# The end of an attention step moved into the next step, and the odd query stacks copied on ScalarE

## The chip, the cores and the metric

The kernel runs on one core of a Trainium2 chip. Its time is the time on the device in microseconds (us). TensorE is called PE here, as in the profile, VectorE DVE, ScalarE ACT, GpSimd POOL and SyncE SP. Each takes its own instructions in their order and waits on semaphores for the others. All DMAs of this kernel are issued by SP.

## The reference

Eight batches of 256 tokens with 128 features go through an adaptive layer norm, an attention block in overlapping windows with a small MLP, a second adaptive layer norm and a soft mixture of eight experts. Cut to what matters here, the attention of one batch is:

```python
x = layernorm(hidden_states, ln1_g, ln1_b)
q, k, v = heads(x @ wq + bq), heads(x @ wk + bk), heads(x @ wv + bv)   # 16 heads of 8
for i in range(0, S, 32):                                              # 8 windows
    start, end = max(0, i - 16), min(S, i + 48)
    attn = softmax(q[:, start:end] * 8 ** -0.5 @ k[:, start:end].T)
    wo = attn @ v[:, start:end]
    out[:, start:end] = blend(out, wo)                                 # linear ramps where windows overlap
out = merge_heads(out) @ wproj + bproj + residual
```

## The kernel before

**Stages.** After a start (modulation of the norm, loads), a loop `step(b)` over the eight batches computes attention on all engines at once; every engine has its own `step(b)`, written by hand as a list of calls. Then come the MLP of all tokens and the experts, which the change leaves alone (from about 216 us on in the profile).

**Scores.** A window has up to 64 tokens. The 16 heads are split in two row groups of the PE array (`par`), the windows in even and odd ones (`eo`), the tokens in two halves (`sel`): eight groups g of 16 small matmuls. q and k are cut into three bf16 parts and stacked as 48 rows, six products of parts at once. The stacks `qst[b % 3][eo]` and `kst[b % 3]` are made by a way through DRAM: ACT copies q and k out of PSUM (`copy_qk`, lines 716 to 722), DVE cuts them into `parts` (`cut_qk`, lines 1063 to 1068), SP writes the parts to `stack_scratch` (`write_parts`, line 266) and reads them back as stacks (`read_stacks`, line 277): two DMAs each for even queries, keys and odd queries. The even and the odd query stack hold the same numbers; they are two because the rows with the maxima differ.

**Two passes.** `scores_a(b, g)` (line 392) computes scores from which DVE takes the negative maxima (`maxima`, line 1073). `cut_m` on POOL cuts these into two bf16 parts, `transpose_m` on PE (line 415) turns them, `copy_mt` on DVE (line 1079) takes them out of PSUM, and `write_mrow` on SP (line 285) writes them with four DMAs as two further rows of the query stack. `scores_b(b, g)` (line 407) computes the transposed scores with the maxima already off; ACT takes `exp` (line 740), `probs_v` (line 430) multiplies with V, `copy_pv` (line 746), `turn_sums` (line 440) and `normalise` on DVE (lines 1087 to 1095) divide by the sums, `gather_context` (line 450) puts the windows together, ACT copies the context (line 803), `project_out` (line 457) projects it and `attention_out` (line 1102) adds the residual. In PE's step b the calls `a(g)` are `scores_a(b + 1, g)`.

**What is ahead of what.** In step b PE turns and projects batch b + 3 (`transpose_x`, `project_qk`, w0b and w1b), and V of batch b + 2 (`project_v`, line 371). The scores of pass a use the banks psa[0] and psa[1] in turn; psa[0] also takes `transpose_m(b, 1)`, so that `scores_a(b + 1, 0)` waits for `mt_ready`. w1b is shared by `project_qk`, `transpose_m(b, 0)`, the gather and the projection. `keep_busy` issues filler matmuls on constants. The end of PE's step before is:

```python
turn_sums(b, 1)
keep_busy(5)
gather_context(b)
scores_b(b + 1, 1)
project_out(b)
```

## Time and profile before

| | us |
|---|---|
| median of 3 runs | 343.5 |
| the runs | 335.82, 343.5, 345.52 |
| the profiled execution | 340.69 |
| its span | 338.9 |
| PE busy in it | 284.3 (84%) |
| DVE, ACT, POOL busy | 224.2, 141.1, 75.3 |

The span runs from the first to the last instruction; the profiled execution's own time is 1.8 us more. Rows of the profile name a line of the kernel, an engine, what it writes and reads, and how often. A busy PE is not PE at its peak; PEclk is the clock it was granted, as a share of 2.4 GHz. Of a row of matmuls that follow each other the start of the next one tells the time it took, since their ends overlap.

### The profile page before, as it was taken

How to read it: one execution, taken by the hardware profiler on the slowest of the kernel's cores; microseconds unless marked ns; L12 is line 12 of the kernel's file. 1: busy time of each engine (PE TensorE's matmuls, PEld its weight loads, DVE VectorE, ACT ScalarE, POOL GpSimd, SP SyncE). 2: the span in 40 equal slices, each digit the busy share in tenths (PEclk: the TensorE clock that was granted, in tenths of full speed). 3: DMA queues.
4: the chain of work that ended last, by engine and by line, in shares of the span. 5: the costliest groups of instructions: out<-in, count | busy, mean ns of one | idle time of the engine just before them, and what ended most of it. 6: DMA issues, size and time to landing. Idle time of an engine off the chain costs nothing.

```text
span 338.9 us, 10357 instructions
## 1 busy us (share of the span) xinstructions
PE 284.3 (84%) x4168; PEld 223.3 (66%) x4168; DVE 224.2 (66%) x634; ACT 141.1 (42%) x282; POOL 75.3 (22%) x116
## 2 busy tenths in 40 slices
PE   4865479599897988969998899887899989999992
PEld 2323356387775766747876787565697779778992
DVE  7554764466758376452645626498857898798986
ACT  1343136328354462734226235654536216624220
POOL 5453240311403141000101010215540024003020
PEclk9775558859789796995558557999989999999999
DMA  6107752377617365271710340000000000101011
GB/s 183 43 0 202 167 120 47 106 164 174 172 35 177 92 122 150 52 186 35 142 22 6 120 143 3 0 2 0 0 2 1 0 2 0 32 2 31 2 32 32
DMA packets 21902, 23.71 MB, mean 70 GB/s; under 512 B 3296, under 2 KB 18528, under 8 KB 21856
## 3 DMA queue, kind: packets, MB, share of 16 engines
q1 hardware_dynamic: 21856, 23.06, 27.2%
q8 instruction: 33, 0.54, 0.7%
q14 instruction: 13, 0.11, 0.1%
HBM read 14.67 MB, written 8.13 MB: 67 GB/s over the span
## 4 chain that ended last, share of the span: by engine, by line
PE 47%; DVE 17%; issue 9%; SPq 8%; DMA 8%; ACT 7%; POOL 2%; ACTq 0%; DVEq 0%; POOLq 0%
PE bank L655 6%; SPq L285 5%; PE bank L407 5%; PE bank L450 4%; DMA qst<-mt 4%; PE bank L371 4%; PE bank L430 3%; PE bank L392 3%; DVE xh L1032 3%; PE bank L440 3%; PE bank L637 3%; PE bank L639 3%; PE bank L638 3%; DVE acc L1371 2%; DMA vmsk<-in_vmask 2%
## 5 line engine op out<-in xcount | busy, mean ns | idle before, releaser
L1073 DVE TENSOR_REDUCE nm<-bank 128x8 f32<-128x512 f32 x64 | 43.6, 688 | 28.3 <-PE bank L392 28.2
L878 POOL TENSOR_TENSOR rs<-ve,mhalf 128x2 f32<-128x2 f32 (+1 forms) x24 | 19.4, 810 | 137.4 <-DVE ve L1029 130.6
L740 ACT ACTIVATE prob<-bank 128x512 f32<-128x512 f32 x64 | 36.6, 600 | 29.1 <-PE bank L407 28.6
L392 PE MATMUL bank<-kst,qst 48*64 48x64 bf16 x1024 | 32.5, 213 | 6.4 <-issue 4.3
L830 ACT ACTIVATE sg<-bank 128x512 f32<-128x512 f32 x32 | 18.9, 601 | 43.5 <-PE bank L639 42.0
L655 PEld LDWEIGHTS bank<-wds,hh 128*128 128x128 f32 x256 | 32.3, 191 | 7.0 <-issue 5.4
L655 PE MATMUL bank<-wds,hh 128*128 128x128 f32 x256 | 33.7, 277 | 2.8 <-DVE acc L1371 2.3
L392 PEld LDWEIGHTS bank<-kst,qst 48*64 48x64 bf16 x1024 | 25.4, 125 | 16.0 <-issue 13.3
L407 PE MATMUL bank<-qst,kst 50*64 50x64 bf16 x1024 | 31.0, 213 | 3.9 <-DMA qst<-mt 3.5
L430 PE MATMUL bank<-prob,vb 128*32 128x64 f32 x1024 | 27.8, 258 | 7.6 <-issue 4.7
L1371 DVE SCALAR_TENSOR_TENSOR acc<-bank,rt,acc 128x128 f32<-128x128 f32 x112 | 32.6, 341 | 1.2
L407 PEld LDWEIGHTS bank<-qst,kst 50*64 50x64 bf16 x1024 | 24.7, 125 | 10.4 <-DMA qst<-mt 4.8
L637 PE MATMUL bank<-h3rest,wpart 128*128 128x512 f32 x64 | 27.5, 430 | 0.8 <-ACT sg L830 0.8
L430 PEld LDWEIGHTS bank<-prob,vb 128*32 128x32 f32 x1024 | 21.3, 130 | 10.4 <-issue 5.7
L1273 DVE TENSOR_TENSOR hh<-sg,bank 128x512 f32<-128x512 f32 x32 | 21.8, 682 | 6.6 <-ACT sg L830 5.8
L639 PE MATMUL bank<-h3part,wpart 128*128 128x512 f32 x64 | 25.1, 393 | 0.0
L638 PE MATMUL bank<-h3part,wrest 128*128 128x512 f32 x64 | 25.1, 392 | 0.0
L347 PE MATMUL bank<-ones 128*128 128x256 bf16 x100 | 22.7, 371 | 2.6 <-issue 2.6
L614 PEld LDWEIGHTS bank<-w2s,gt 128*128 128x128 f32 x128 | 17.9, 209 | 7.1 <-issue 5.0
L1032 DVE TENSOR_SCALAR xh<-xs,mv,rs 128x128 f32<-128x128 f32 x32 | 15.7, 535 | 6.6 <-POOL rs L878 6.6
L614 PE MATMUL bank<-w2s,gt 128*128 128x128 f32 x128 | 18.4, 295 | 1.0 <-DVE comb L1242 1.0
L1102 DVE TENSOR_TENSOR res<-bank,res 128x256 f32<-128x256 f32 x8 | 3.4, 425 | 23.7 <-PE bank L457 23.7
(140 smaller groups left out, 498.8 us busy)
## 6 DMA issues: line engine op xcount, KB each, us to landing
qst<-stack_scratch SPq DMA_DIRECT2D x32, 216.0 KB, 4.8
stack_scratch<-parts SPq DMA_DIRECT2D x16, 216.0 KB, 2.5
kst<-stack_scratch SPq DMA_DIRECT2D x16, 216.0 KB, 5.0
stack_scratch<-parts SPq DMA_DIRECT2D x16, 144.0 KB, 2.4
stack_scratch<-parts SPq DMA_DIRECT2D x16, 72.0 KB, 2.1
qst<-mt SPq DMA_DIRECT2D x64, 4.0 KB
out_x<-fin SPq DMA_DIRECT2D x4, 256.0 KB, 2.3
xs<-in_x SPq DMA_DIRECT2D x1, 896.0 KB, 7.2
```

Of the source, the lines that this page charges most:

```text
L392: m = pe.matmul(psa[g % 2][WIN * half:WIN * half + WIN, WIN * h2:WIN * h2 + WIN], qst[n][eo][rows_, h2, at:at + WIN], kst[n][rows_, h2, at ...
L407: m = pe.matmul(bank[WIN * half:WIN * half + WIN, WIN * h2:WIN * h2 + WIN], kst[n][rows_, h2, at:at + WIN], qst[n][eo][rows_, h2, at:at + ...
L430: m = pe.matmul(psv[32 * ct:32 * ct + 32, at:at + WIN], vb[n][:, eo, H2 * par + h2, sel, :, :], prob[par][:, h2, sel, :], start=True, stop ...
L614: m = pe.matmul(bk[6][:, k * P:(k + 1) * P], gt[:, c, k * P:(k + 1) * P], w2s[:, c, :], start=(c == 0 and k == 0), stop=(c == FF - 1), ski ...
L637: pe.matmul(bank[:], wpart[:, w, e, :], tokens_rest, start=True, stop=False)
L638: pe.matmul(bank[:], wrest[:, w, e, :], tokens, start=False, stop=False)
L639: return pe.matmul(bank[:], wpart[:, w, e, :], tokens, start=False, stop=True)
L655: m = pe.matmul(bk[4 + e % 2][:, k * P:(k + 1) * P], hh[e][:, k * P:(k + 1) * P], wds[:, e, :], start=True, stop=True)
L740: act.activation(prob[g // 2 % 2][:, :, g % 2, :], psb[g % 2][:].rearrange("p (h q) -> p h q", h=H2), ACT.Exp).then_inc(exp_done, 1)
L1032: return dve.tensor_scalar(dst, src, mean, r, ALU.subtract, ALU.mult)
L1073: dve.tensor_reduce(nm[:, g, :], psa[g % 2][:].rearrange("p (h k) -> p h k", h=H2), AX_X, ALU.max, negate=True).then_inc(max_done, 1)
L1371: dve.scalar_tensor_tensor(out=acc[:, k, :], in0=src, scalar=w, in1=acc[:, k, :], op0=ALU.mult, op1=ALU.add).then_inc(acc_step, 1)
```

## The change

It moves `gather_context(b)`, the copy of the context, `project_out(b)` and `attention_out(b)` from the end of step b into step b + 1 (and behind the loop for the last batch). `project_v` is done one batch ahead instead of two, in the middle of the step, `transpose_x(b + 3)` and `project_qk(b + 3)` come later, `copy_qk(b + 3)` becomes ACT's last call of the step and `cut_qk(b + 3)` DVE's last. SP writes the parts one step later, and sends the second half's maxima rows ahead of the stack reads. The odd query stack is not read from the scratch: ACT copies it from the even one in two pieces (`copy_odd`), for which DVE fills 32 rows of each even stack with zeros at the start, three fills more. Some waits of PE that were repeated in each group are made once. Fillers go from 9 to 6 in a step.

The diff, without the declaration of the semaphore:

```diff
@@ -269,8 +270,7 @@
                 n = b % DEEP
                 if b >= DEEP:
                     sp.wait_ge(b_done, after(b_done, 8 * (b - DEEP + 1)))
-                for k, stack, written in ((0, qst[n][0], q_written), (1, kst[n], k_written),
-                                          (0, qst[n][1], q_written)):
+                for k, stack, written in ((0, qst[n][0], q_written), (1, kst[n], k_written)):
                     sp.wait_ge(written, after(written, 48 * (b + 1)))
                     rows_of = scr[b, k].rearrange("t (d h) n -> (t d) h n", h=NH)
                     for r in range(2):
@@ -298,7 +298,7 @@
                 sp.dma_start(dst[:], src).then_inc(small_loaded, 16)
 
             write_parts(0)
-            sp.wait_ge(ones_ready, after(ones_ready, 2 * DEEP))
+            sp.wait_ge(ones_ready, after(ones_ready, 3 * DEEP))
             read_stacks(0)
             write_parts(1)
             write_mrow(0, 0)
@@ -315,16 +315,12 @@
 
             def step(b):
                 write_mrow(b, 1)
-                if b == 0:
-                    write_parts(2)
-                elif b + 2 < B:
-                    read_stacks(b + 2)
+                if b + 2 < B:
+                    write_parts(b + 2)
                 if b + 1 < B:
                     write_mrow(b + 1, 0)
-                if b == 0:
-                    read_stacks(2)
-                if b + 3 < B:
-                    write_parts(b + 3)
+                if b + 2 < B:
+                    read_stacks(b + 2)
                 if b == B - 2:
                     load_late()
 
@@ -379,11 +375,13 @@
 
             def scores_a(b, g):
 
-                pe.wait_ge(stack_ready, after(stack_ready, 96 * (b + 1)))
                 if g == 0:
+                    pe.wait_ge(stack_ready, after(stack_ready, 64 * (b + 1)))
                     pe.wait_ge(mt_ready, after(mt_ready, 2 * b))
                 else:
                     pe.wait_ge(max_done, after(max_done, 8 * b + g - 1))
+                if g == 4:
+                    pe.wait_ge(odd_ready, after(odd_ready, 2 * (b + 1)))
                 par, halves = spans(g)
                 eo, n = g // 4, b % DEEP
                 rows_ = slice(64 * par, 64 * par + ROWS)
@@ -396,7 +394,8 @@
 
             def scores_b(b, g):
 
-                pe.wait_ge(mrow_ready, after(mrow_ready, 128 * b + 64 * (g // 4 + 1)))
+                if g % 4 == 0:
+                    pe.wait_ge(mrow_ready, after(mrow_ready, 128 * b + 64 * (g // 4 + 1)))
                 if g:
                     pe.wait_ge(exp_done, after(exp_done, 8 * b + g - 1))
                 par, halves = spans(g)
@@ -419,7 +418,8 @@
             def probs_v(b, gp):
                 n = b % 2
                 pe.wait_ge(exp_done, after(exp_done, 8 * b + 2 * gp + 2))
-                pe.wait_ge(v_ready, after(v_ready, 4 * (b + 1)))
+                if gp == 0:
+                    pe.wait_ge(v_ready, after(v_ready, 4 * (b + 1)))
                 eo, par = gp // 2, gp % 2
                 if par == 0:
                     pe.wait_ge(pvs_ready, after(pvs_ready, 2 * b + eo))
@@ -521,17 +521,14 @@
             transpose_x(2)
             for g in range(5, 8):
                 scores_a(0, g)
+            keep_busy(6)
+            scores_b(0, 0)
+            scores_b(0, 1)
             pe.wait_ge(mt_ready, after(mt_ready, 1))
             project_qk(2)
-            pe.wait_ge(qk_ready, after(qk_ready, 12))
-            project_v(1, 0)
-            project_v(1, 1)
-            keep_busy(10)
-            scores_b(0, 0)
-            scores_b(0, 1)
 
             def step(b):
-                ahead, prep, values = b + 1 < B, b + 3 < B, b + 2 < B
+                ahead, prep = b + 1 < B, b + 3 < B
 
                 def a(g):
                     if ahead:
@@ -543,41 +540,42 @@
                 probs_v(b, 0)
                 scores_b(b, 3)
                 a(0)
-                keep_busy(2)
+                if b + 2 < B:
+                    pe.wait_ge(qk_ready, after(qk_ready, 4 * (b + 3)))
+                if b:
+                    gather_context(b - 1)
+                if ahead:
+                    project_v(b + 1, 0)
+                    project_v(b + 1, 1)
+                else:
+                    turn_tokens(0)
                 a(1)
+                probs_v(b, 1)
+                if b:
+                    project_out(b - 1)
+                scores_b(b, 4)
+                a(2)
+                scores_b(b, 5)
+                a(3)
+                turn_sums(b, 0)
+                if ahead:
+                    keep_busy(3)
                 if prep:
                     pe.wait_ge(v_ready, after(v_ready, 4 * (b + 2)))
                     transpose_x(b + 3)
-                a(2)
-                if not ahead:
-                    turn_tokens(0)
-                probs_v(b, 1)
-                if prep:
-                    pe.wait_ge(att_ready, after(att_ready, b))
-                    project_qk(b + 3)
-                a(3)
-                scores_b(b, 4)
-                scores_b(b, 5)
-                turn_sums(b, 0)
-                keep_busy(2)
                 a(4)
+                pe.wait_ge(att_ready, after(att_ready, b))
                 if ahead:
-                    if prep:
-                        pe.wait_ge(qk_ready, after(qk_ready, 4 * (b + 4)))
-                    else:
-                        pe.wait_ge(att_ready, after(att_ready, b))
                     transpose_m(b + 1, 0, w1b)
                 else:
                     turn_tokens(1)
                 probs_v(b, 2)
                 scores_b(b, 6)
-                if values:
-                    pe.wait_ge(v_ready, after(v_ready, 4 * (b + 2)))
-                    project_v(b + 2, 0)
                 a(5)
+                if prep:
+                    pe.wait_ge(mt_ready, after(mt_ready, 2 * b + 3))
+                    project_qk(b + 3)
                 scores_b(b, 7)
-                if values:
-                    project_v(b + 2, 1)
                 a(6)
                 if not ahead:
                     turn_tokens(2)
@@ -587,23 +585,19 @@
                 else:
                     pe.wait_ge(late_loaded, after(late_loaded, 128))
                     first(0, 0)
+                a(7)
+                turn_sums(b, 1)
                 if ahead:
-                    pe.wait_ge(mt_ready, after(mt_ready, 2 * b + 3))
+                    keep_busy(3)
+                    scores_b(b + 1, 1)
                 else:
                     first(0, 1)
-                    pe.wait_ge(att_ready, after(att_ready, b))
-                a(7)
-                turn_sums(b, 1)
-                keep_busy(5)
-                gather_context(b)
-                if ahead:
-                    scores_b(b + 1, 1)
-                else:
-                    first(0, 2)
-                project_out(b)
 
             for b in range(B):
                 step(b)
+            gather_context(B - 1)
+            first(0, 2)
+            project_out(B - 1)
 
             def second(g, c):
 
@@ -739,6 +733,19 @@
                 act.wait_ge(pv_done, after(pv_done, 4 * b + g // 2 - 1))
                 act.activation(prob[g // 2 % 2][:, :, g % 2, :], psb[g % 2][:].rearrange("p (h q) -> p h q", h=H2),
                                ACT.Exp).then_inc(exp_done, 1)
+
+            def copy_odd(b, half):
+
+                act.wait_ge(stack_ready, after(stack_ready, 64 * (b + 1)))
+                heads = slice(H2 // 2 * half, H2 // 2 * (half + 1))
+                even, odd = [qst[b % DEEP][eo][0:64 + ROWS, heads, LINE - S:LINE] for eo in range(2)]
+                act.activation(odd, even, ACT.Copy).then_inc(odd_ready, 1)
+
+            def copy_ctxt(b):
+                act.wait_ge(ctx_done, after(ctx_done, b + 1))
+                act.wait_ge(proj_done, after(proj_done, b))
+                act.activation(ctxt[:], w1b[:, PAD:PAD + S], ACT.Identity, bias=col[:, BV:BV + 1]
+                               ).then_inc(ctxt_ready, 1)
 
             def copy_pv(b, eo):
                 act.wait_ge(pv_done, after(pv_done, 4 * b + 2 * eo + 2))
@@ -770,25 +777,31 @@
             copy_qk(1)
             copy_mod(7, bk[1])
             copy_v(0)
+            copy_odd(0, 0)
+            copy_odd(0, 1)
             copy_xt(2)
-            copy_qk(2)
-            copy_v(1)
             exp(0, 0)
             exp(0, 1)
+            copy_qk(2)
 
             def step(b):
                 ahead, prep = b + 1 < B, b + 3 < B
                 exp(b, 2)
+                if b:
+                    copy_ctxt(b - 1)
                 exp(b, 3)
-                if prep:
-                    copy_xt(b + 3)
                 if not ahead:
                     copy_h2t(0)
                 copy_pv(b, 0)
+                if ahead:
+                    copy_odd(b + 1, 0)
+                exp(b, 4)
+                if ahead:
+                    copy_v(b + 1)
+                    copy_odd(b + 1, 1)
+                exp(b, 5)
                 if prep:
-                    copy_qk(b + 3)
-                exp(b, 4)
-                exp(b, 5)
+                    copy_xt(b + 3)
                 if not ahead:
                     copy_h2t(1)
                 exp(b, 6)
@@ -796,19 +809,15 @@
                 copy_pv(b, 1)
                 if not ahead:
                     copy_h2t(2)
-                if ahead:
+                else:
                     exp(b + 1, 0)
-                act.wait_ge(ctx_done, after(ctx_done, b + 1))
-                act.wait_ge(proj_done, after(proj_done, b))
-                act.activation(ctxt[:], w1b[:, PAD:PAD + S], ACT.Identity, bias=col[:, BV:BV + 1]
-                               ).then_inc(ctxt_ready, 1)
-                if ahead:
                     exp(b + 1, 1)
-                if b + 2 < B:
-                    copy_v(b + 2)
+                if prep:
+                    copy_qk(b + 3)
 
             for b in range(B):
                 step(b)
+            copy_ctxt(B - 1)
 
             def copy_h3t(g, bank):
                 act.wait_ge(t3_done, after(t3_done, g + 1))
@@ -958,13 +967,13 @@
                     cut_m(b + 1, 0)
                 if group is not None:
                     root_tokens(group)
-                if b + 3 < B:
-                    copy_x1v(b + 3)
                 if b + 4 < B:
                     norm_x(b + 4)
                     second_root_x(b + 4)
                 if b + 1 < B:
                     cut_m(b + 1, 1)
+                if b + 3 < B:
+                    copy_x1v(b + 3)
 
             for b in range(B):
                 step(b)
@@ -1134,6 +1143,7 @@
             for n in range(DEEP):
                 for par in range(2):
                     dve.memset(kst[n][64 * par + 32:64 * par + 64].bitcast(F32), TWO_ONES).then_inc(ones_ready, 1)
+                dve.memset(qst[n][0][32:64].bitcast(F32), 0.0).then_inc(ones_ready, 1)
 
             dve.wait_ge(sc_exp, after(sc_exp, 1))
             dve.tensor_scalar(sce[:, 1, :], sce[:, 0, :], 1.0, None, ALU.add).then_inc(sc_step, 1)
@@ -1196,41 +1206,41 @@
                 copy_mt(b, 1)
                 maxima_next(0)
                 maxima_next(1)
+                if b:
+                    attention_out(b - 1)
                 if norm:
                     ln_a(b + 4)
+                if group is not None:
+                    ln2_stats(group)
                 maxima_next(2)
                 if norm:
                     ln_b(b + 4)
                 maxima_next(3)
-                if group is not None:
-                    ln2_stats(group)
                 normalise(b, 0)
                 if ahead:
                     copy_mt(b + 1, 0)
                 maxima_next(4)
-                if prep:
-                    cut_qk(b + 3, 0)
-                maxima_next(5)
-                if prep:
-                    cut_qk(b + 3, 1)
                 if group is not None:
                     normed_tokens(group)
-                maxima_next(6)
+                maxima_next(5)
                 if not ahead:
                     gate(GA)
                 if norm:
                     ln_c(b + 4)
+                maxima_next(6)
                 maxima_next(7)
                 normalise(b, 1)
                 if norm:
                     ln_d(b + 4)
-                attention_out(b)
-                if not ahead:
-                    ln2_stats(NG - 1)
+                if prep:
+                    cut_qk(b + 3, 0)
+                    cut_qk(b + 3, 1)
 
             for b in range(B):
                 step(b)
 
+            attention_out(B - 1)
+            ln2_stats(NG - 1)
             normed_tokens(NG - 1)
             gate(GB)
```

## Rows read from the trace of the kernel before

**Rows 1.** Windows by step: us; busy PE, PEld, DVE, ACT, POOL; PEclk; DMA share; GB/s

```profile
54.90:78.10 23.20, 18.47 (x442) 14.62 (x438) 12.79 (x34) 9.33 (x21) 4.79 (x10) 0.78 0.51 123
78.10:158.50 80.40, 68.52 (x1730) 53.86 (x1729) 48.92 (x123) 40.66 (x91) 16.45 (x35) 0.86 0.49 119
158.50:179.40 20.90, 20.37 (x427) 16.63 (x425) 10.43 (x30) 7.05 (x14) 1.92 (x5) 0.56 0.34 68
179.40:199.00 19.60, 17.61 (x429) 14.32 (x422) 10.76 (x31) 7.02 (x14) 1.93 (x5) 0.61 0.33 108
```

**Rows 2.** The page: granted clock in 40 equal slices of the span, in tenths

```profile
PEclk9775558859789796995558557999989999999999
```

**Rows 3.** Timeline of PE in step 2: start us, us, engine, line, tiles, [idle before it]

```profile
104.80 0.65 PE L430 MATMUL bank<-prob,vb 128*32 128x64 f32 x32 [0.58 <-ACT prob L740]
105.38 0.44 PE L407 MATMUL bank<-qst,kst 50*64 50x64 bf16 x16
105.75 0.71 PE L371 MATMUL bank<-wa,x1v 128*128 128x128 f32 x4
...
110.55 0.47 PE L430 MATMUL bank<-prob,vb 128*32 128x64 f32 x17 [2.20 <-issue]
...
113.49 2.08 PE L450 MATMUL bank<-idf,ctxn 128*128 128x128 f32 x8
...
116.13 0.71 PE L457 MATMUL bank<-wa,ctxt 128*128 128x128 f32 x4 [0.15 <-ACT ctxt L803]
```

**Rows 4.** Timeline of PE in steps 5 and 6, at the lower clock

```profile
161.97 1.08 PE L430 MATMUL bank<-prob,vb 128*32 128x64 f32 x32
...
168.09 0.63 PE L407 MATMUL bank<-qst,kst 50*64 50x64 bf16 x16
168.65 1.22 PE L371 MATMUL bank<-wa,x1v 128*128 128x128 f32 x4
```

**Rows 5.** The chain of waits in order of time: start us, us, what

```profile
4.99 6.84 DMA vmsk<-in_vmask
...
201.76 1.77 DMA qst<-mt
...
213.69 1.16 PE bank L450 x8
```

**Rows 6.** Timeline of DVE, start, batch 2's cut and step 2

```profile
9.30 0.29 DVE L1055 COPY scb<-sce 128x256 f32<-128x256 f32 x1
...
48.98 0.76 DVE L1063 TENSOR_TENSOR qkr<-qk,parts 128x576 f32<-128x576 f32 x1 [2.36 <-ACT parts L722]
...
50.27 0.76 DVE L1068 TENSOR_TENSOR parts<-qkr,parts 128x576 bf16<-128x576 f32 x1
...
97.59 0.28 DVE L1079 COPY mt<-bank 32x256 bf16<-32x256 bf16 x1 [0.16 <-PE bank L415]
```

**Rows 7.** Timeline of SP's issues in step 2

```profile
97.89 2.69 SPq L285 DMA_DIRECT2D qst<-mt  x4
...
103.10 0.88 SPq L277 DMA_DIRECT2D qst<-stack_scratch  x2
...
108.75 3.04 SPq L266 DMA_DIRECT2D stack_scratch<-parts  x6
```

**Rows 8.** Groups by line and form: count, busy us, mean ns, idle ahead of them

```profile
L734 ACT ACTIVATE vb<-bank 64x256 f32<-64x256 f32 x32 | 12.0, 376 | 4.4 <-PE bank L371 3.8
...
L746 ACT ACTIVATE pvs<-bank 128x512 f32<-128x512 f32 x16 | 9.6, 597 | 20.5 <-PE bank L430 20.5
...
L1136 DVE MEMSET kst<- 32x1152 f32 x6 | 6.1, 1018 | 2.5 <-issue 1.5 <-PEq L1475 1.0
```

**Rows 9.** Timeline of ScalarE in step 2, the copies of q and k

```profile
102.09 0.50 ACT L716 ACTIVATE qk<-bank,bqs 128x288 f32<-128x288 f32 x1 [0.89 <-PE bank L363]
...
103.26 0.51 ACT L722 ACTIVATE parts<-bank,col 128x288 bf16<-128x288 f32 x1
```

**Rows 10.** DMA issues by line: KB each, median us to landing

```profile
qst<-stack_scratch SPq DMA_DIRECT2D x32, 216.0 KB, 4.8
```

1 line of the change is left out of this document (added).

## The prediction

> **What bounds the kernel now.** I read first the busy shares by step and then the orders of the queues inside one step. The table of windows [rows 1] cuts the attention loop at the starts of `transpose_m(b,1)`: step 0 takes 23.2 us, steps 1 to 4 take 80.4, 20.1 each, step 5 takes 20.9 and step 6 takes 19.6. PE is busy 80 to 97% of these rows while no other engine reaches 65%, and its granted clock is 0.56 to 0.86 on the mean: it falls towards 1.2 GHz again and again [rows 1, 2]. So a step is PE's fixed order of work, and what lengthens it is any wait in that order and the clock that is lost after it.
>
> The rows of one step show both. Back to back at 2.4 GHz a score group starts 0.37 after the one before, `probs_v` takes 0.58, a half of `project_v` 0.64 [rows 3]; the same at 1.2 GHz take 0.56, 1.0 and 1.15 [rows 4], and the gather 1.16 against 2.08 [rows 3, 5]. In step 2 PE stands still for 2.20 before 110.55, and the gather at 113.49 runs at the lower clock [rows 3]. That tail (turn the sums, divide, gather, copy, project) is a chain through four engines with 9 filler matmuls per step beside it.
>
> Two transfers bind the order of a step. A half of the maxima goes `transpose_m`, `copy_mt` on DVE (0.28) [rows 6], four DMA issues in a row on SP (2.69) [rows 7], 1.77 to land [rows 5], then `scores_b`. From the start of `copy_mt` that is 0.28 + 2.69 + 1.77 + about 0.05 for hand-overs = 4.8 us.
>
> **The change, part by part.**
>
> *The tail.* The gather and output projection of step b-1 leave the end and stand between `a(0)` and `scores_b(b,4)`. What stood alone on PE there was gather, context copy wait and projection, 1.16 + 0.5 + 0.64 at 2.4 GHz; from 110.55 to the next step 6.6 us passed in step 2 [rows 3]. Now the tail after `scores_b(b+1,0)` is `a(7)`, sums, three fillers, `scores_b(b+1,1)`, about 1.7 us.
>
> *What comes in the way: the cut of q and k.* Before, ScalarE copied qk(b+3) in mid-step and DVE cut it between maxima. Now `copy_qk(b+3)` stands behind `exp(b+1,1)`, the last exponential of the step, and both `cut_qk` calls are DVE's last work of the step. DVE's next instruction is `copy_mt(b+1,1)`. It is queued behind the cut, and behind it wait `a(0)` of step b+1, since bank psa[0] comes free only with `mt_ready`, and on SP the maxima rows for `scores_b(b+1,4)`. The exponential takes 0.6, as the copy of the same 512 columns [rows 8]. The four copies of `copy_qk` take from 102.09 to 103.77, 1.7 [rows 9]. The cut takes from 48.98 to 51.03, 2.05 [rows 6]. With 0.1 of hand-overs, `copy_mt` starts 4.45 after the end of `scores_b(b+1,1)` and ends at 4.75. PE has `scores_b(b+1,2)`, `transpose_m`, `probs_v`, `scores_b(b+1,3)` for this time, 0.37 + 0.16 + 0.58 + 0.37 = 1.5, and stands still for about 3.1. This falls in steps 0 to 5, since batches 2 to 7 are cut so.
>
> *The new step.* Let `a(0)` start at 0, with `copy_mt` just ended.
> - PE to `scores_b(b,4)`: 0.37 + 1.16 + 1.28 + 0.37 + 0.58 + 0.64 = 4.4. The maxima rows: 2.69 + 1.77 + 0.05 = 4.5. So 4.5; the moved work is hidden exactly, at 2.4 GHz. At 1.2 GHz it is 0.56 + 2.0 + 2.3 + 0.56 + 1.0 + 1.15 = 7.6 and not hidden.
> - ScalarE then has in a row: `exp(b,4)`, `copy_v` (4 x 0.39 apart, about 1.6), `copy_odd` second half, and `a(4)` waits for this copy. The odd copy of 4 heads by 256 columns is 1,024 elements in bf16; the trace has none of that size. Copies of 256 take 376 ns and of 512 take 597 [rows 8], a slope of 0.86 ns: 1.04 us. Bounds: 0.8, if it were two copies of 512 that start as close together as those of `copy_qk`, 0.39 [rows 9]; and 1.5, four copies of 256 without overlap. I take 1.0, the line through the two sizes, since only source and destination change. `scores_b(b,4)` ends at 4.9; 4.9 (the first half ends at 5.3) + 0.5 + 1.6 + 1.0 = 8.4 for `a(4)`. PE gets there with b(4), a(2), b(5), a(3), sums, fillers and the transposes of x at about 7.3, so a second stop of 1.1.
> - `transpose_m(b+1,0)` 0.4 later, 0.25 to its result and 4.8 of copy and rows: `scores_b(b+1,0)` at 13.9. PE's own work there is 4.4 and one exponential, so a stop of about 0.7.
> - tail of 1.7 to `scores_b(b+1,1)`, its own 0.37: 16.0. Then 4.75 as above: 20.7.
>
> So even at full clock a step takes 20.7, as long as now (20.1).
>
> *The clock.* Each step now has one gap of 3.1 us and stops of 1.1 and 0.7. In the trace a gap of 2.20 was enough for the gather at 113.49 to run at 1.2 GHz [rows 3], and steps 5 and 6, with least work, stand at 0.56 and 0.61 [rows 1]; in step 2 it is back for the projection at 116.13. I take the lower clock for the stretch after the gap, up to `scores_b(b,4)`: 7.6 instead of 4.5, +3.1, of which 0.2 goes back into shorter stops. Forecast 23.6 a step. Bounds: 20.7 with the clock up throughout; all at 1.2 GHz 7.6 to `scores_b(b,4)`, 3.6 over ScalarE to `a(4)`, 7.5 of PE work to `scores_b(b+1,0)`, 3.2 to the end of `scores_b(b+1,1)` and 4.7 for copy and cut: 26.6.
> The Trainium skill, "TensorE: Matmul & The Clock Gate", section "HAM oscillation — how this bites in real kernels", tells of a kernel in which a DMA wait that recurs in every tile makes TensorE pay its warm-up again in every tile. It speaks against this change: by it each of these steps would be a 23.6 one, without it each 20.7. The trace of before agrees in that every step has a stretch at half clock.
>
> *Odd stacks not read.* Two of six stack reads per batch go, 2 x 216 KB [rows 10] and 0.9 us of SP issue [rows 7] each time. They lie beside other work, since the reads are a step ahead. At the start it counts, where the first score group waits for all six: 0.9 of issue, and about as much in the landing, as a third of what is under way goes; I book -1.8.
>
> *Order on SP.* `write_parts(b+2)` (3.04 of issue [rows 7]) stands between the two rows groups: SP is free again 6.1 after `a(0)`, the second group's maxima are there at 9.4. No cost. The stack reads follow at 12.1 to 13.9 and land 4.8 later [rows 10], 2 us ahead of the next `a(0)`; only behind step 5, where no cut delays `a(0)`, would they be 1.1 late. Dropped PE waits and the later `copy_x1v` cost nothing: what they waited for is long done in each case.
>
> *The start.* DVE gets three more fills of 32x1152. One takes 1.02, and the six of before have 2.5 of idle ahead of them [rows 8], 1.0 of it ahead of the first, so 0.3 each: 3.9 us. `spread_sc` at 9.30 [rows 6], which feeds the first modulation matmul, slips by it. Some of that was covered by a wait for a load that ended at 11.83 [rows 5]; I book +2.9. With the -1.8 above: +1.1. Bounds 0 and +3.9.
>
> **The sum.** Profiled execution: 340.7 (span 338.9 and 1.8 around it).
> - start: +1.1
> - step 0: no gather in it, 20.4 at full clock, 22.5 with part at half, against 23.2 from one `copy_mt` to the next: -0.7
> - steps 1 to 4: 4 x (23.6 - 20.1) = +14.0
> - steps 5 to 7: without the cut behind them 18.9 and 17.8 at full clock, 22.7 at half; they were mostly at half and are of equal work (one gather and one `project_v` more, 15 fillers less): +0.5
>
> 355.6. The median shown (343.5) is 0.8% above the profiled execution, so the median may stand above the sum; I say 356.
>
> **Rivals.**
> - *Clock lost as little as now.* Before has the same kind of loss with its mean of 0.86 in steps 1 to 4. If a step is 21.9: 340.7 + 1.1 - 1.3 + 7.2 - 1 = 347. For it: the gather and `project_v` after the gap are long matmuls, as those ahead of 116.13 in step 2, where it came back [rows 3]. Against: more idle per step than now. Chance 0.17.
> - *Everything at 1.2 GHz.* 26.6 a step, 22.7 in steps 5 and 6: 340.7 + 1.1 + 1.8 + 26.0 + 4.9 = 374. Step 5 of before is nearly that [rows 1]. Chance 0.20.
> - *The other side: faster.* The moved tail keeps PE dense and the clock stays at 2.4 GHz to the end of step 6: steps 20.4, 4 x 20.7, 18.9, 17.8. Then 340.7 + 1.1 - 2.8 + 2.4 - 2.0 - 1.8 - 0.6 = 337, 1.1% under. It decides the case if the steps without a cut behind them run at 0.9 clock or more and the odd copy takes under 0.8. A little more of either gives over 2%. Chance 0.11.
> - *DVE lets `copy_mt` past the waiting cut.* Then the block would not exist and a step would be about 17. Nothing in the trace shows an instruction of DVE out of order, so it has no chance of its own.
> The Trainium skill, "TensorE: Matmul & The Clock Gate", section "Architectural detail: the array is 16× 32×32, not 1× 128×128", says the same: VectorE and ScalarE are strictly first in, first out.
>
> **The numbers.** Forecast as above 0.52, its own range 348 to 364 (steps of 22 to 25.5). With the rivals: range 344 to 371, which leaves out the faster case and the upper part of the one at 1.2 GHz, under 0.2. About 2% is what a measurement of this kernel tells from no change: below 336.6 0.05; 336.6 to 350.4 (the rest of the faster case, most of the first rival, the low end of the forecast) 0.23; slower 0.72.
>
> **What would show it.** In the profile after: `copy_mt(b,1)` right behind `cut_qk` on DVE, and PE idle of about 3 us before the first score group of the next batch in steps 0 to 5, absent in step 6; an odd copy of about 1.0 us; PE waiting for it before the fifth score group; the context copy waiting for little; PE's clock under 0.8 in steps 1 to 4; the first modulation matmul near 13.6. I am wrong if the gap is under 2 us, if steps 1 to 4 take under 21, or if the start is not later.

## The result, and the profile after

| | before | after |
|---|---|---|
| median, us | 341.24 (4 runs, 335.82 to 345.52) | 357.37 (4 runs, 356.39 to 357.53) |
| the profiled execution | 340.69 | 357.48 |
| its span | 338.9 | 355.6 |
| PE busy | 284.3 (84%) | 282.1 (79%) |
| mean granted clock | 0.832 | 0.791 |

The kernel after takes 1.059 times as long as before, interval 1.050 to 1.068: slower. The runs of before spread by 3%, and the ratios here and below leave disturbed runs out, so that a ratio need not be that of the two medians.

PE does as much work as before and waits longer for it. First the windows, cut like [rows 1] at `copy_mt(b,1)`, step 0, steps 1 to 4, step 5 and step 6 (length; busy PE, PEld, DVE, ACT, POOL; PEclk; DMA share; GB/s):

```profile
56.20:79.80 23.60, 18.61 (x416) 14.60 (x416) 12.35 (x35) 11.02 (x22) 4.78 (x10) 0.59 0.31 79
79.80:175.70 95.90, 76.35 (x1712) 61.29 (x1712) 48.37 (x124) 47.86 (x96) 15.65 (x35) 0.68 0.31 78
175.70:195.00 19.30, 15.26 (x374) 12.98 (x374) 10.23 (x31) 8.84 (x17) 1.87 (x5) 0.68 0.37 94
195.00:215.20 20.20, 16.83 (x423) 14.34 (x422) 10.28 (x30) 9.42 (x19) 1.87 (x5) 0.67 0.18 53
```

Steps 1 to 4 take 24.0 us each where they took 20.1, at a clock of 0.68 where it was 0.86. That is 15.4 of the 16.8 us between the two profiled executions. Of the rest, the start up to `copy_mt(0,1)` is 1.0 longer (56.21 against 55.25), step 0 is 0.5 longer, steps 5 and 6 are 1.0 shorter, and what comes behind them is 0.9 longer. The page's clock line (one digit for each fortieth of the span, to be compared with [rows 2]) tells the same:

```profile
PEclk9596558557868558576585765999999999999999
```

The list of waits of the kernel after (who waited for whom: us in total, times, longest) names the first cause:

```profile
PE bank L390 <- DVE mt L1088: 14.6, 6, 2.9
...
PE bank L390 <- ACT qst L742: 8.1, 7, 2.4
...
PE bank L352 <- ACT vb L728: 6.5, 5, 1.8
...
PE bank L406 <- DMA qst<-mt: 2.8, 4, 1.0
```

L390 is `scores_a`. Six times, ahead of `a(0)` of steps 0 to 5, PE stands for `copy_mt` on DVE, 2.4 us on the mean; seven times it stands for the odd copy (L742), 1.2 on the mean. `transpose_x` (L352) waits for the copies of V (L728), which nobody had forecast; it lies right before the wait for the odd copy. DVE's timeline around the end of step 1 (start us, us) shows what is ahead of `copy_mt`, to be compared with [rows 6]:

```profile
100.60 0.76 DVE L1072 TENSOR_TENSOR qkr<-qk,parts 128x576 f32<-128x576 f32 x1 [1.34 <-ACT parts L716]
101.39 0.46 DVE L1075 CAST parts<-qkr 128x576 bf16<-128x576 f32 x1
101.89 0.76 DVE L1077 TENSOR_TENSOR parts<-qkr,parts 128x576 bf16<-128x576 f32 x1
102.56 0.27 DVE L1088 COPY mt<-bank 32x256 bf16<-32x256 bf16 x1
```

DVE first waits for the last copy of q and k on ScalarE (L716), cuts, and only then takes the maxima out of PSUM. The same stretch and the next step on PE, to be compared with [rows 3]:

```profile
99.64 0.44 PE L406 MATMUL bank<-qst,kst 50*64 50x64 bf16 x16
102.98 0.64 PE L390 MATMUL bank<-kst,qst 48*64 48x64 bf16 x16 [2.90 <-DVE mt L1088]
103.55 2.07 PE L450 MATMUL bank<-idf,ctxn 128*128 128x128 f32 x8
105.42 1.91 PE L367 MATMUL bank<-wa,x1v 128*128 128x128 f32 x8
107.26 0.63 PE L390 MATMUL bank<-kst,qst 48*64 48x64 bf16 x16
...
108.51 0.71 PE L457 MATMUL bank<-wa,ctxt 128*128 128x128 f32 x4
...
112.20 0.44 PE L352 MATMUL bank<-idf,x1h 128*128 128x128 f32 x2 [1.19 <-ACT vb L728]
113.37 0.44 PE L390 MATMUL bank<-kst,qst 48*64 48x64 bf16 x16 [0.73 <-ACT qst L742]
...
118.57 1.08 PE L430 MATMUL bank<-prob,vb 128*32 128x64 f32 x32 [0.27 <-ACT prob L734]
...
127.34 0.64 PE L390 MATMUL bank<-kst,qst 48*64 48x64 bf16 x16 [2.28 <-DVE mt L1088]
```

Before the gap a score group takes 0.44 and behind it 0.64; the gather takes 2.07, which is its time at 1.2 GHz (1.16 at 2.4 GHz, [rows 5]). The clock is back at 108.51 (the projection takes 0.71), and gone again at 118.57 (`probs_v` 1.08 instead of 0.65), some 5 us behind the two stops on ScalarE.

### The profile page after: what moved, and what is told of

Read it like the earlier page. It is cut to its first block, busy times and chain, and to the rows that moved or that the text cites. A ratio compares the mean times of both kernels' runs of the same rounds, so it can differ in the third digit from the quotient of the medians.

```text
span 355.6 us, 10179 instructions
## 1 busy us (share of the span) xinstructions
PE 282.1 (79%) x4134; PEld 223.9 (63%) x4134; DVE 227.0 (64%) x637; ACT 155.9 (44%) x298; POOL 74.0 (21%) x116
## 3 DMA queue, kind: packets, MB, share of 16 engines
q1 hardware_dynamic: 20832, 19.52, 20.5%
## 4 chain that ended last, share of the span: by engine, by line
PE 45%; DVE 21%; ACT 12%; issue 12%; DMA 4%; POOL 3%; SPq 3%; ACTq 0%; DVEq 0%; POOLq 0%
PE bank L649 6%; PE bank L390 4%; PE bank L450 4%; PE bank L430 4%; DVE xh L1041 4%; PE bank L406 4%; PE bank L367 3%; ACT qst L742 3%; PE bank L631 3%; PE bank L633 3%; PE bank L632 3%; SPq L285 3%; DMA qst<-mt 2%; PE bank L358 2%; ACT vb L728 2%
## 5 line engine op out<-in xcount | busy, mean ns | idle before, releaser
L390 PE MATMUL bank<-kst,qst 48*64 48x64 bf16 x1024 | 33.7, 220 | 26.4 <-DVE mt L1088 14.6
L734 ACT ACTIVATE prob<-bank 128x512 f32<-128x512 f32 x64 | 37.4, 597 | 36.6 <-PE bank L406 36.3
L887 POOL TENSOR_TENSOR rs<-ve,mhalf 128x2 f32<-128x2 f32 (+1 forms) x24 | 19.5, 814 | 137.2 <-DVE ve L1038 135.4
L390 PEld LDWEIGHTS bank<-kst,qst 48*64 48x64 bf16 x1024 | 27.4, 132 | 31.2 <-issue 24.6
L406 PEld LDWEIGHTS bank<-qst,kst 50*64 50x64 bf16 x1024 | 25.6, 133 | 15.0 <-issue 9.8
L430 PE MATMUL bank<-prob,vb 128*32 128x64 f32 x1024 | 29.0, 274 | 3.4 <-ACT prob L734 2.7
L430 PEld LDWEIGHTS bank<-prob,vb 128*32 128x32 f32 x1024 | 22.6, 142 | 7.4 <-ACT prob L734 6.7
L932 POOL CAST mp<-nm 128x32 bf16<-128x32 f32 x16 | 3.3, 209 | 85.1 <-DVE nm L1082 85.1
L753 ACT ACTIVATE pvs<-bank 128x512 f32<-128x512 f32 x16 | 9.6, 597 | 25.5 <-PE bank L430 25.5
L608 PEld LDWEIGHTS bank<-w2s,gt 128*128 128x128 f32 x128 | 16.3, 192 | 7.1 <-issue 5.0
L747 ACT ACTIVATE ctxt<-bank,col 128x256 f32<-128x256 f32 x8 | 3.8, 473 | 33.7 <-PE bank L450 33.7
```

Of the source, the lines that this page charges most:

```text
L390: m = pe.matmul(psa[g % 2][WIN * half:WIN * half + WIN, WIN * h2:WIN * h2 + WIN], qst[n][eo][rows_, h2, at:at + WIN], kst[n][rows_, h2, at ...
L406: m = pe.matmul(bank[WIN * half:WIN * half + WIN, WIN * h2:WIN * h2 + WIN], kst[n][rows_, h2, at:at + WIN], qst[n][eo][rows_, h2, at:at + ...
L430: m = pe.matmul(psv[32 * ct:32 * ct + 32, at:at + WIN], vb[n][:, eo, H2 * par + h2, sel, :, :], prob[par][:, h2, sel, :], start=True, stop ...
L734: act.activation(prob[g // 2 % 2][:, :, g % 2, :], psb[g % 2][:].rearrange("p (h q) -> p h q", h=H2), ACT.Exp).then_inc(exp_done, 1)
```

## The experiments

Steps are taken from one `copy_mt(b,1)` on DVE to the next. The kernels of one group shared their runs of before.

### The cut of q and k put behind the maxima rows

```diff
                 copy_mt(b, 1)
                 maxima_next(0)
+                if b + 2 < B:
+                    cut_qk(b + 2, 0)
+                    cut_qk(b + 2, 1)
                 maxima_next(1)
...
-                if prep:
-                    cut_qk(b + 3, 0)
-                    cut_qk(b + 3, 1)
```

> The changed kernel with one thing moved: DVE cuts q and k of batch b + 2 in step b, behind copy_mt(b,1) and the first maxima, not at the end of step b - 1 ahead of them. ScalarE's order is as in the changed kernel. Theory (the cut that waits for copy_qk holds copy_mt, and with it a(0) and the rows of maxima): the gap of PE before the first score group of the next batch, 2.4 us on the mean in six steps, goes, and copy_mt(b,1) follows transpose_m at once. At full clock the step loses 3 to 4 us; steps 1 to 4 take 19 to 21.5 instead of 24.0, the whole 337 to 345. Rival (the odd copies on ScalarE and the lower clock make the step long, the gap is only where it shows): the wait moves to the fifth score group or to the rows of maxima and steps 1 to 4 stay above 23, the whole 352 or more.

Measured: 339.27 us (338.39 to 341.88), beside 342.07 of before in the same group; ratio 1.011 with an interval of 0.991 to 1.031. The wait of `scores_a` for `mt` is no longer in the list, that for the odd copy is (8.0, 7 times). Steps 1 to 4 take 20.5 each in place of 24.0. DVE's timeline of this kernel:

```profile
93.34 0.27 DVE L1088 COPY mt<-bank 32x256 bf16<-32x256 bf16 x1
95.57 0.69 DVE L1082 TENSOR_REDUCE nm<-bank 128x8 f32<-128x512 f32 x1 [1.95 <-PE bank L390]
96.18 0.75 DVE L1072 TENSOR_TENSOR qkr<-qk,parts 128x576 f32<-128x576 f32 x1
```

The copy goes at once, and the cut is done while PE works. The order of three calls on DVE is worth 18 us of the kernel after. By the medians that is more than the whole loss, by the ratios (from 1.059 to 1.011) most of it.

The clock is higher without the gap, 0.79 in steps 1 to 4 instead of 0.68, but it still falls at the same place. PE's timeline around the end of step 1:

```profile
93.55 0.44 PE L406 MATMUL bank<-qst,kst 50*64 50x64 bf16 x16
94.89 0.64 PE L390 MATMUL bank<-kst,qst 48*64 48x64 bf16 x16 [0.90 <-DMA kst<-stack_scratch]
95.46 2.07 PE L450 MATMUL bank<-idf,ctxn 128*128 128x128 f32 x8
```

The gather takes its time at 1.2 GHz here too, behind a stop of 0.90. In steps 1 to 7 of this kernel it never takes less than 1.91. So a slow gather is not by itself a sign of the long gap.

### Filler matmuls in the gap

How much of these 18 us is the gap itself, and how much the clock behind it? Ten fillers were put where PE stands still. They add nothing to the result, and `a(0)` starts no earlier for them.

```diff
                 scores_b(b, 3)
+                if b + 2 < B:
+                    keep_busy(10)
                 a(0)
```

> The changed kernel with ten filler matmuls more in steps 0 to 5, between scores_b(b,3) and a(0), where PE otherwise stands still for 2.3 to 2.9 us: 10 fillers are 1.3 us at 2.4 GHz and 2.3 at 1.2, so they add nothing to the path. Theory (of the 24.0 us of a step 3 are what the lower clock costs behind the gap): PE's clock is higher in the stretch behind the gap, steps 1 to 4 take 21 to 22.5, the whole 348 to 352. Rival (the clock follows from the whole step's waits, or those times are set by transfers and copies): the step stays within 0.5 of 24.0 and the whole within 2 us of the changed kernel.

Measured: 347.49 us (345.15 to 350.39), ratio 1.030 (1.011 to 1.050): 9.9 us less than the kernel after, by more work. The profiled execution was the slowest of the four. PE's timeline at the same place:

```profile
96.81 1.26 PE L343 MATMUL bank<-ones 128*128 128x256 bf16 x10
99.78 0.44 PE L390 MATMUL bank<-kst,qst 48*64 48x64 bf16 x16 [1.70 <-DVE mt L1090]
100.15 1.16 PE L450 MATMUL bank<-idf,ctxn 128*128 128x128 f32 x8
```

`copy_mt` is as late as before, but the idle time is cut from 2.90 to 1.70, and the gather behind it takes 1.16 instead of 2.07. It is so in two of the six gaps (the other is at 120.73). In the other four PE comes at the lower clock already, the ten fillers take 2.32, about the length of the gap, and the gathers behind them take 1.86 to 2.07. The clock does not rise in every step. Steps 0 and 2 are short now, 20.8 and 20.95 us at 0.83 and 0.92, where they took 23.6 and 24.4 at 0.59 and 0.64 in the kernel after. Steps 1, 3 and 4 still take 23.1 to 23.9, step 4 at 0.64 as there.

So what the fillers give back is clock, since they shorten no wait. The 9.9 us of the medians is only a rough size for it: this execution is 7.1 us shorter than that of the kernel after, and 1.1 of that is there at `copy_mt(0,0)` (43.23 against 44.38), ahead of the first filler. What is left of the 18.1 comes with the idle time itself, 14.6 in all, part of which goes into the waits that come next.

### The odd stacks read from the scratch again

```diff
-                for k, stack, written in ((0, qst[n][0], q_written), (1, kst[n], k_written)):
+                for k, stack, written in ((0, qst[n][0], q_written), (1, kst[n], k_written),
+                                          (0, qst[n][1], q_written)):
...
-                    copy_odd(b + 1, 0)
...
-                    copy_odd(b + 1, 1)
...
-                dve.memset(qst[n][0][32:64].bitcast(F32), 0.0).then_inc(ones_ready, 1)
```

> The changed kernel with the odd query stacks read from the scratch again: six stack reads for a batch, no copies of the odd stack on ScalarE, no fills of the even stacks on DVE. All else as changed. Theory (the odd copies cost 3.9 of fills at the start of which 2.9 show, less 1.8 gained in the first reads, and 1 us in each step between scores_b(b,4) and a(4)): start 1 us earlier, step 1 us shorter, in sum 6 to 8 us less, 349 to 351. Rival (the reads lie on the path and the copies are hidden): as slow as the changed kernel or slower, above 356.

Measured: 349.97 us (348.6 to 351.5), ratio 1.039 (1.021 to 1.057). The time is the one expected, the way to it is not. The kernel has a new first wait, and none for `mt`:

```profile
PE bank L388 <- DMA qst<-stack_scratch: 27.0, 7, 4.8
```

and SP's timeline shows where it comes from, beside PE's first score group of the next batch:

```profile
109.46 2.69 SPq L285 DMA_DIRECT2D qst<-mt  x4
112.25 0.83 SPq L277 DMA_DIRECT2D qst<-stack_scratch  x2
113.13 0.89 SPq L277 DMA_DIRECT2D kst<-stack_scratch  x2
114.06 0.89 SPq L277 DMA_DIRECT2D qst<-stack_scratch  x2
...
121.55 0.64 PE L388 MATMUL bank<-kst,qst 48*64 48x64 bf16 x16 [4.62 <-DMA qst<-stack_scratch]
```

The last read is issued at 114.95 and has landed 6.6 later, when six reads are under way instead of four. In the new order of SP the stack reads stand behind the second half's maxima rows, and with the odd ones among them they are the last thing that `a(0)` waits for. So this experiment swapped one gap for another: steps 1 to 4 fell only from 24.0 to 23.0, the start and step 0 together by 7.2, and steps 5 and 6 grew by 5.1. It doesn't price the odd copy alone, which the next one does.

### The odd copies on GpSimd, two batches ahead

The stacks are not read from the scratch, as in the kernel after; GpSimd copies them at the end of its own step, so ScalarE has neither copy nor wait.

```diff
                 if b + 3 < B:
                     copy_x1v(b + 3)
+                if b + 2 < B:
+                    copy_odd(b + 2, 0)
+                    copy_odd(b + 2, 1)
```

> The changed kernel with the copies of the odd stacks on GpSimd, which has nothing to do for most of a step, instead of ScalarE, at the end of its step b for batch b + 2. Theory (the second odd copy stands in the chain from scores_b(b,4) over exp, copy_v to the fifth score group and costs about 1 us a step, 7 steps): PE's wait before that group goes, steps 1 to 4 take 22.5 to 23.3 instead of 24.0, the whole 349 to 353. Rival (it is copy_v, not the odd copy, that holds this place, or the lower clock eats it): within 2 us of the changed kernel. If a copy takes over 4 us there, GpSimd's cut of the maxima is late and the kernel is slower than the changed one.

Measured: 352.39 us (349.92 to 355.0), ratio 1.041 (1.033 to 1.050): 5.0 less than the kernel after. Part of what the two copies cost on ScalarE comes back as a longer gap, since PE comes to the block of copy and cut earlier:

```profile
PE bank L390 <- DVE mt L1090: 19.3, 6, 3.9
```

It was 14.6. One copy takes on either engine (groups by line: count, busy, mean ns, idle ahead; the kernel after first, then this one):

```profile
L742 ACT ACTIVATE qst<-qst 112x1024 bf16<-112x1024 bf16 x16 | 16.7, 1052 | 0.2
```

```profile
L920 POOL COPY qst<-qst 112x1024 bf16<-112x1024 bf16 x16 | 18.1, 1159 | 21.5 <-DMA kst<-stack_scratch 21.5
```

### The fills of the even stacks, later and elsewhere

First the three fills of DVE were put later, ahead of the first cut that came late enough.

```diff
             ln_a(2)
             ln_b(2)
+            fill_even(0)
+            fill_even(1)
+            fill_even(2)
             cut_qk(1, 0)
```

> The changed kernel with the three fills of the even stacks moved from the head of DVE's list to behind ln_b(2), where DVE waits for ScalarE anyway. Theory (2.9 of the fills' 3.8 us show at the start, booked +2.9): the first modulation matmul is back near 9.7 us instead of 13.5, the first maxima rows come 2.5 to 3 us earlier, the steps stay at 24.0, the whole 354 to 355. Rival (the start waits for loads and the first stacks, so the fills are covered): under 1 us less.

Measured: 357.0 us (356.04 to 357.86), ratio 1.053 (1.046 to 1.059), no difference to the kernel after. The first modulation matmul came back to 9.74, but this edit was badly placed: the fills now ran from 27.91 to 31.34, and SP's first stack reads, which wait for them, were issued only at 31.37. The first score group started at 38.17, as in the kernel after (38.38). It says nothing on the term it was meant for. So the fills were given to GpSimd, which has nothing to do from 5.1 to 14.4 us.

```diff
-                dve.memset(qst[n][0][32:64].bitcast(F32), 0.0).then_inc(ones_ready, 1)
...
+            for n in range(DEEP):
+                pool.wait_ge(consts_pool, after(consts_pool, 5 + n))
+                pool.memset(qst[n][0][32:64].bitcast(F32), 0.0).then_inc(consts_pool, 1)
```

> The kernel after the change, with the three fills of the even query stacks done by POOL instead of DVE. POOL stands still from 5.1 to 14.4 us there, and one of its fills of 128x2048 takes 1.8, so three of 32x1152 fit in without being seen. First theory (the fills of the prediction's start term, 2.9): the first modulation matmul goes back from 13.46 to about 9.7, the first score group from 38.4 to about 35.5, the first copy of maxima from 44.38 to about 41.5, the whole from 357.4 to about 354.5. Rival (what follows the first matmul was covered by later waits, for loads, stacks or instructions): the first matmul goes back, the first score group stays within 1 us of 38.4, the whole 356.5 to 357.5.

Measured: 355.45 us (354.47 to 356.7), ratio 1.046 (1.039 to 1.052). PE's first modulation matmul, its first score group, and DVE's first `copy_mt(0,0)` in this kernel (its L348 is the modulation, L391 `scores_a`):

```profile
9.73 2.86 PE L348 MATMUL bank<-wms,scb 128*128 128x512 f32 x4 [3.10 <-DVE scb L1068]
...
34.77 1.06 PE L391 MATMUL bank<-kst,qst 48*64 48x64 bf16 x32 [1.18 <-issue]
```

```profile
40.48 0.28 DVE L1092 COPY mt<-bank 32x256 bf16<-32x256 bf16 x1 [0.26 <-PE bank L415]
```

In the kernel after they stand at 13.46, 38.38 and 44.38: 3.7, 3.6 and 3.9 later. The first theory holds at the start. How much of the fills is covered there is not settled, since the start itself differs between executions: `copy_mt(0,0)` stands at 44.38 in the kernel after and at 43.23 in the one with fillers in the gap, which has the same start, and at 40.48 here and 41.33 in the kernel with all three repairs. That is 1.9 to 3.9, 2.9 expected. In the whole only 1.9 us is left. The lead is still 3.6 at `copy_mt(1,1)` (76.18 against 79.80) and 2.1 at `copy_mt(2,1)` (100.49 against 102.56). The windows of that step 1, first the kernel after, then this one, show that here it ran at the lower clock for longer, 0.71 against 0.80:

```profile
79.80:102.56 22.76, 17.00 (x428) 13.71 (x428) 12.71 (x35) 11.92 (x24) 4.84 (x10) 0.80 0.33 82
```

```profile
76.18:100.49 24.31, 18.89 (x428) 15.16 (x428) 12.79 (x36) 11.98 (x24) 4.78 (x10) 0.71 0.31 77
```

### All three repairs together

The cut behind the rows, the odd copies on GpSimd and the fills on GpSimd.

> The kernel after the change with three repairs at once: the cut of q and k behind the copy of the maxima rows (alone it gave 339.3), the odd stacks copied by POOL (alone it gave 352.4, 5.0 less than the kernel after) and the fills by POOL. If the causes add up: 339.3 - 5.0 = 334.3, less 0 to 2.9 for the fills: 331 to 335. If the first repair had already hidden the copies of ScalarE, or the clock takes back what they give: 337 to 340.

Measured: 331.87 us (329.54 to 337.24), beside 341.53 of before in the same group; ratio 0.976 (0.970 to 0.982). The single repairs gave 18.1, 5.0 and 1.9, together 25.0; the three at once give 25.5. So within the spread of the runs the causes add up, and what is left of the change is 2.4% faster than before. Steps 1 to 4 take 19.5 each.

### The tail alone

The other way round: the kernel before, with nothing but the moved tail, which also takes the place of two fillers (order of reads, cuts, odd stacks and `project_v` as they were).

```diff
                 scores_b(b, 3)
                 a(0)
-                keep_busy(2)
+                if b:
+                    gather_context(b - 1)
                 a(1)
...
                 a(2)
+                if b:
+                    project_out(b - 1)
...
                 keep_busy(5)
-                gather_context(b)
                 if ahead:
                     scores_b(b + 1, 1)
-                else:
-                    first(0, 2)
-                project_out(b)
```

> The kernel before with only the end of the step moved: gather after a(0) (in place of two fillers), context copy after exp(b,2), projection after a(2), residual after the second maximum, all one step later; cut, copies of q, k and v, transfers and fillers at the end as before. Theory (moving the tail is a gain by itself, what follows it in the change is what costs): from 20.1 a step to 17 to 18.5, 7 steps, the whole 322 to 332. Rival (what was gained at the end is lost where the moved work stands, since project_qk now waits for the projection's bank and the rows of maxima still set the pace): within 2% of the kernel before.

Measured: 328.46 us (325.96 to 335.86), ratio 0.974 (0.952 to 0.995). Measured again with more runs, since this interval was wide:

> The kernel before with only the tail moved, once more and in more rounds, since its first interval reached from 0.952 to 0.995. If the tail alone is worth what the first runs showed: 326 to 332 beside about 341 of before. If the first runs were lucky: within 1% of before.

Measured: 332.47 us (326.27 to 338.15), ratio 0.966 (0.958 to 0.975). The part of the change that it was named for is worth 3.4%. Its interval overlaps that of the kernel with the three repairs, so which of them is the faster stays open. Steps 1 to 4 take 19.4 each in the first profiled execution and 18.7 in the second, more than the 17 to 18.5 of the theory, though the whole came in at or near its 322 to 332. PE's timeline in step 2 of the first has the moved work (L450, L457) back to back with its neighbours at 2.4 GHz, and no wait there for the divided context or its copy (other steps of this execution, like that of the gather at 135.60 with 2.07, are at the lower clock):

```profile
113.25 0.44 PE L392 MATMUL bank<-kst,qst 48*64 48x64 bf16 x16
113.62 1.16 PE L450 MATMUL bank<-idf,ctxn 128*128 128x128 f32 x8
114.71 0.44 PE L392 MATMUL bank<-kst,qst 48*64 48x64 bf16 x16
115.08 0.44 PE L356 MATMUL bank<-idf,x1h 128*128 128x128 f32 x2
115.44 0.44 PE L392 MATMUL bank<-kst,qst 48*64 48x64 bf16 x16
115.81 0.71 PE L457 MATMUL bank<-wa,ctxt 128*128 128x128 f32 x4
```

### Fewer fillers behind the moved tail

```diff
                 turn_sums(b, 1)
-                keep_busy(5)
+                keep_busy(1)
```

> The same kernel with the tail moved, and with one filler matmul instead of five at the end of a step. The five start 0.13 us apart at 2.4 GHz, ahead of the second score group of the next batch. If PE's order of work bounds the step there, four less save 0.5 in each of 7 steps: 3 to 4 us less than the kernel with five. Rival: the idle time that comes in their place costs the clock, and it takes the same time or up to 4 us more.

Measured: 333.72 us (330.81 to 340.58), ratio 0.981 (0.972 to 0.989). It saves nothing and by the ratios it is more likely a loss of some 1.4%; the intervals (0.958 to 0.975 with five) just meet. The rival is nearer.

### The tail with the odd stacks copied

Does the tail alone gain more when a third of the stack reads goes? Once with the copies on ScalarE, behind `exp(b,6)` and `copy_pv(b,1)`, once on GpSimd, both two batches ahead.

> As g3_tail_odd_pool, but the odd stacks are copied on ScalarE, behind exp(b,6) and behind copy_pv(b,1). Two copies of 1.05 us a step stand ahead of exp(b,7) and of exp(b+1,0). Theory: where ScalarE waits for PE anyway the copies are covered in part; 0 to 1 us a step more than on GpSimd, 320 to 332. Rival (ScalarE's order sets the pace wherever the copies stand): 1.5 us a step or more over g3_tail_odd_pool, 332 or more.

> The kernel before with the tail moved (as in t1_tail_only) and in addition the odd stacks copied on GpSimd two batches ahead, not read from the scratch; fills of the even stacks behind ln_b(2). The cut stays in mid-step. Theory (odd copies are free where the engine is idle, and a third fewer stack reads take some of the stops in which PE waits for nothing that the profile names): 318 to 326, and the runs agree more closely than the 326 to 336 of t1_tail_only. Rival (the reads were hidden and cost nothing): 326 to 330 with the same spread.

Measured on ScalarE: 334.25 us (327.76 to 340.05), ratio 0.985 (0.972 to 0.998). On GpSimd: 332.15 us (327.27 to 333.49), ratio 0.970 (0.958 to 0.982), a copy at 1038 ns. Neither comes out faster than the tail alone, so the 318 to 326 of the theory was missed. But the traces do not show that the reads were hidden. In the loop of the tail alone PE stands 8.2 us with no releaser that the profile names (3.18 before 126.24 and 4.11 before 167.58 are the longest), with GpSimd's copies 0.52. And from `copy_mt(0,1)` to `copy_mt(7,1)` it takes 132.7 us with GpSimd's copies, 138.4 and 135.8 in the two executions of the tail alone. Against this stands the start. The fills lie where they lay in the badly placed edit above, the first stack reads are issued at 32.41 instead of 28.07, and the first score group comes at 39.30 instead of 36.83:

```profile
39.30 1.06 PE L394 MATMUL bank<-kst,qst 48*64 48x64 bf16 x32 [4.71 <-issue]
```

What fewer reads are worth with the fills on GpSimd was not tried. Between the two engines the intervals overlap, and it stays open whether ScalarE's copies cost anything. In step 0 one did: the copy stood 6.6 us for a stack that had not landed, and PE 5.2 us for the exponential queued behind it.

## Why the prediction came out right

The median is 357.4, the forecast was 356 with 344 to 371. By its steps:

**The block of copy and cut: right, to half a microsecond.** Forecast: from the end of `scores_b(b+1,1)` 4.75 to the end of `copy_mt`. Measured around 98.3 to 102.83: that group ends just ahead of `exp(b+1,1)` at 98.41, and 4.4 follow. The idle time was forecast at 3.1 in each of steps 0 to 5; it is 2.9 where PE comes to it at 2.4 GHz (at 102.98) and 2.3 where it comes at 1.2 GHz (at 127.34), for then its own work before the gap takes longer. The mean is 2.4. (By the prediction's own numbers, 4.75 less 1.5, it would be 3.25.) As forecast there is none in step 6, where no cut stands ahead: `a(0)` at 196.94 waits 0.16, for a stack read. With the cut moved away the loss is gone, so this is the cause, and not only its sign.

**The length of a step: 23.6 forecast, 24.0 measured, by terms that shifted.** The step from `a(0)` at 102.98 to the next at 127.34, cut where the prediction cut it:

| stretch | forecast at 2.4 GHz | measured | more |
|---|---|---|---|
| `a(0)` to `scores_b(b,4)` | 4.5 | 6.2 (to 109.15) | 1.7 |
| to `a(4)` | 3.9 | 4.2 (to 113.37) | 0.3 |
| to `scores_b(b+1,0)` | 5.5 | 6.2 (to 119.59) | 0.7 |
| to the next `a(0)` | 6.8 | 7.8 | 1.0 |
| sum | 20.7 | 24.4 | 3.7 |

(A mean step of steps 1 to 4 takes 24.0, since step 1 took 22.8.) The prediction put the whole price of the clock, 3.1, into the first row. It is 1.7 there, since the clock is back by 108.51, behind the gather and `project_v`; the rest comes mostly at the end of the step, where the clock has fallen again behind the two stops on ScalarE. The size of the price was right: step 2 with fillers in the gap takes 20.95 at a clock of 0.92, beside 20.7 forecast at full clock. The place was not, and that less idle time than forecast (2.4 for 3.1) and more lost clock came to nearly the forecast sum is in part luck. The Trainium skill, "TensorE: Matmul & The Clock Gate", section "HAM oscillation — how this bites in real kernels", tells of a wait that recurs in each tile and of a warm-up paid each time. The runs agree in that the clock is lost anew in each step and that it rose when the gap was filled or removed. But with the gap gone the gather still takes 2.07, behind a stop of 0.90, so the gap is not the only place where it is lost.

**The odd copy: right.** 1.05 us where 1.0 was taken from the line through two sizes in [rows 8], and waits for it of 1.2 on the mean where 1.1 was forecast. (The 8.4 for `a(4)` is the sum from 5.3, the end of the first half; from the 4.9 written first it would be 8.0.) In five steps another 1.3 stands ahead of it, `transpose_x` for the copies of V in the same queue of ScalarE (L728). The prediction had named these copies as what `a(4)` waits behind and had overlooked that `transpose_x`, ahead of `a(4)` in PE's order, waits for them too; it moves no time, since `a(4)` had to wait anyway. The Trainium skill, "ScalarE: Activation LUTs", section "What ACT_TABLE_LOAD costs", gives 186 ns and 0.833 ns a column for an instruction with immediate scale and bias. That makes an estimate of 1039 for 1024 columns; the trace agrees with 1052.

**The clock in steps 1 to 4: right.** Under 0.8 was forecast, it is 0.68.

**SP's order at no cost: right for this kernel, with less behind it than it seemed.** The part writes took 5.1 of issue in step 2 and not 3.04, so that SP was free 8.1 after `a(0)` and not 6.1, still ahead of `copy_mt(b+1,0)`. The reads are issued by 118.94 and would be in by about 123.5 at the 4.6 us of the median read of keys, 3.8 ahead of the `a(0)` at 127.34 (forecast 2); behind step 5, where 1.1 late was forecast, PE waits 0.16. But with six reads in the same order they are the bound of every step, 3.9 us of waiting in each. What makes the order harmless is that the odd reads are gone, and that the block of DVE delays `a(0)`. With the block repaired the reads show again: 6.1 us in 5 waits for `kst` in the kernel with three repairs. The prediction treated the two edits on their own.

**The start: right in the sum, its terms not settled.** `copy_mt(0,1)` is 1.0 later, 1.1 was forecast. The first modulation matmul came at 13.46 (forecast near 13.6). Of the fills' 3.9 us the prediction booked 2.9, believing that a wait for a load covers 1.0. The first modulation matmul slips by 3.7, so nothing is covered there; at `copy_mt(0,0)` moving the fills to GpSimd gives back 1.9 to 3.9, by the executions compared, with 2.9 in the middle. The missing reads cannot be read off much better: the first score group stands at 36.6 to 37.8 in before and in three profiled executions with the tail moved, which have its start, and at 34.6 and 34.8 in the two with the fills on GpSimd, 1.9 to 3.2 earlier where 1.8 was booked, and the prologue's new order is in this too. Between the two halves the kernel after wins another microsecond: `copy_mt(0,1)` follows 11.8 behind `copy_mt(0,0)` instead of 12.9. What brings this was not tried. That the sum came out to 0.1 is luck, since the same start differs by 1.1 between two executions.

**Step 0: wrong by 1.2.** It was to be 0.7 shorter and is 0.5 longer: its clock is 0.59 over the whole step, and the prediction had let it run at the lower clock in part only.

**Steps 5 to 7: right in the sum.** Forecast 0.5 more; steps 5 and 6 are 1.0 shorter, all behind them 0.9 longer, in sum 0.1 less.

**The rivals.** The one at 347 (less clock lost) and the one at 374 (all at 1.2 GHz) did not come; the clock's 0.68 is between them. Nor did the faster one at 337. "DVE lets `copy_mt` past" got no chance, rightly, but its price was wrong: a step of 17 us without the block. Measured without it: 20.5, and 19.5 with all three repairs. The prediction had taken away the gap and the lost clock and had not asked what is late next: in the kernel with three repairs these are the stack reads, the cut maxima on GpSimd (5.5 us in 7 waits) and the maxima rows (4.9 in 7).

## What to carry to other kernels

When work is moved, read the queue of each engine it passes and ask what short instruction now stands behind a long one: three calls of DVE in the wrong order cost 18 us, more than the moved tail alone brings (3.4%, some 12 us). Split a change that has several parts before judging it: its main idea was worth 3.4% alone, and three side edits (cut last, copy on a loaded engine, fills ahead of the first product) took 25 us from it. Idle time on TensorE can be paid twice, as time and as clock: the same step took 20.95 us at a clock of 0.92 and 24.4 at 0.64. And place an edit like the fills by what waits for it: in three kernels here they held up the first stack reads, and the start lost what the edit was to gain.
